# The broadcast of 1/l in a fused attention and gated-scan kernel, issued from ScalarE's queue instead of SyncE's

## What is computed

```python
x = x + attention(layernorm(x))      # x: 32 batches, 256 tokens, 128 channels
x = x + scan_ffn(layernorm(x))

# attention: 16 heads of 64, 4 persistent keys and values ahead of the 256
h = rms_norm(x) * norm_weight
q, k, v = split(h @ w_qkv.T)
q, k = rope(q), rope(k)
scores = einsum('bhid,bhjd->bhij', q, concat(pm_k, k)) * 64 ** -0.5
attn = softmax(where(causal, scores, min))
out = einsum('bhij,bhjd->bhid', attn, concat(pm_v, v)) @ w_out.T

# scan_ffn: the 32 batches are the steps of a scan
f, i = sigmoid(x_t @ wf.T + c @ uf.T + bf), sigmoid(x_t @ wi.T + c @ ui.T + bi)
c = f * c + i * tanh(x_t @ wc.T + c @ uc.T + bc)
h = tanh(x @ wo.T + c_final @ uo.T + bo)
```

## Time and profile before

| | us |
|---|---|
| median of three runs | 1159.35 (1157.94 to 1163.04) |
| the profiled execution | 1162.89 |
| its span, first to last instruction | 1161.0 |
| TensorE busy in it | 1088.0 (94%) |
| VectorE busy | 951.9 (82%) |
| ScalarE busy | 707.2 (61%) |
| GpSimd busy | 649.2 (56%) |

### The profile page before, as it was taken

The page is one execution under the profiler, slowest core; times in us unless marked ns, Lnnn a source line. Parts: engine busy times, 40 slices in busy tenths (PEclk is TensorE's granted clock), DMA queues, the critical chain, the costliest instruction groups (busy, mean ns, idle before and its releaser), DMA issues.

```text
span 1161.0 us, 47269 instructions
## 1 busy us (share of the span) xinstructions
PE 1088.0 (94%) x18411; PEld 826.2 (71%) x18411; DVE 951.9 (82%) x3304; ACT 707.2 (61%) x1603; POOL 649.2 (56%) x828
## 2 busy tenths in 40 slices
PE   4879999999999999999999999999999999999981
PEld 2557777777777777777777777777777777777671
DVE  6678888888878988888888888888888888888646
ACT  3556666666556566656666666666666566666634
POOL 3545555556555555655555565555646555655415
PEclk8799999999999999999999999999999999999995
DMA  6213333332333333233333323333332233333205
GB/s 204 93 71 99 112 112 112 112 112 77 96 110 107 113 112 99 90 98 112 105 112 113 110 86 93 110 112 113 112 112 90 85 108 108 108 107 107 72 2 145
DMA packets 78031, 120.52 MB, mean 104 GB/s; under 512 B 13041, under 2 KB 35954, under 8 KB 77682
## 3 DMA queue, kind: packets, MB, share of 16 engines
q1 hardware_dynamic: 68722, 111.21, 31.3%
q10 hardware_dynamic: 9088, 6.29, 2.0%
HBM read 41.56 MB, written 8.78 MB: 43 GB/s over the span
## 4 chain that ended last, share of the span: by engine, by line
PE 57%; DVE 15%; DMA 14%; SPq 5%; issue 4%; POOL 4%; ACT 2%; DVEq 0%; POOLq 0%; ACTq 0%
PE bank_pv L1081 10%; DMA rope_c<-rope_b 10%; PE bank L974 9%; PE bank_st L1037 7%; PE bank_sum L1118 6%; PE bank_sum L1102 4%; PE bank_sm L1013 4%; DMA linv_scratch<-linv 3%; DVE masked L781 3%; PE bank L996 3%; SPq L298 2%; DVE linv L804 2%; PE bank L993 2%; PE bank L1204 2%; PE bank L1206 2%
## 5 line engine op out<-in xcount | busy, mean ns | idle before, releaser
L396 POOL TENSOR_TENSOR qk<-rope_a,rope_c 128x512 f32<-128x512 f32 x256 | 340.7, 1331 | 304.8 <-DMA rope_c<-rope_b 300.8
L781 DVE CUSTOM_DVE_ANT_0 masked<-bank_sm,mask_q 128x132 bf16<-128x132 f32 (+1 forms) x1024 | 307.6, 356 | 44.2 <-PE bank_sm L1013 43.4
L389 POOL TENSOR_TENSOR prob<-prob 128x264 f32<-128x264 f32 x256 | 212.0, 828 | 157.6 <-ACT prob L535 150.7
L535 ACT ACTIVATE prob<-bank_st 128x784 f32<-128x784 f32 x256 | 210.3, 822 | 115.3 <-PE bank_st L1046 114.3
L770 DVE TENSOR_TENSOR rope_a<-bank,cos 128x512 f32<-128x512 f32 x256 | 174.3, 681 | 102.1 <-PE bank L974 74.6
L520 ACT ACTIVATE qk_h<-qk 128x512 f16<-128x512 f32 x256 | 160.2, 626 | 128.9 <-POOL qk L396 128.6
L1081 PE MATMUL bank_pv<-prob,v_sb 128*64 128x256 f32 (+1 forms) x2048 | 224.7, 340 | 0.6 <-DVE raw L797 0.6
L1037 PE MATMUL bank_st<-qk 64*64 64x196 f32 (+3 forms) x4096 | 185.7, 298 | 0.1
L771 DVE TENSOR_TENSOR rope_b<-bank,sin 128x512 f32<-128x512 f32 x256 | 173.8, 679 | 0.0
L1037 PEld LDWEIGHTS bank_st<-qk 64*64 64x64 f32 x4096 | 167.3, 133 | 9.0 <-issue 0.8
L1081 PEld LDWEIGHTS bank_pv<-prob,v_sb 128*64 128x64 f32 x2048 | 124.3, 136 | 54.3 <-issue 0.8
(11 more groups left out here) (202 smaller groups left out, 1793.7 us busy)
## 6 DMA issues: line engine op xcount, KB each, us to landing
rope_c<-rope_b SPq DMA_DIRECT2D x512, 128.0 KB, 2.1
rinv<-linv_scratch SPq DMA_DIRECT2D x124, 256.0 KB, 4.5
out<-x_sb SPq DMA_DIRECT2D x16, 256.0 KB, 2.5
linv_scratch<-linv SPq DMA_DIRECT2D x62, 64.0 KB, 2.1
x_sb<-x ACTq DMA_DIRECT2D x28, 128.0 KB, 5.3
pre<-w_qkv_t ACTq DMA_DIRECT2D x1, 1024.0 KB, 5.3
v_sb<-pm_v SPq DMA_DIRECT2D x64, 8.0 KB
v_end<-v_end_scratch SPq DMA_DIRECT2D x64, 8.0 KB
```

The source lines that it names most:

```text
L389: G.tensor_tensor(prob_2[:, s % 4, :, :], prob[:, s % 4, :, 0:NT - Q1], prob[:, s % 4, :, C0 + Q1:SCOL], ALU.add).then_inc(S["prob_added"], 1)
L396: G.tensor_tensor(qk[:, s, :].rearrange("p (u n) -> p u n", u=2)[:, :, 0:NT], rope_a[:, (NPAIR * j + s) % 3, :].rearrange("p (u n) -> p u ...
L535: A.activation(prob[:, s % 4, :, :], ps_st[:, :, 0:SCOL], ACT.Exp).then_inc(S["exp_done"], 1)
L781: ins = V.tensor_tensor_reduce(masked[:, e, c0:c0 + n], ps_sm[:, e, c0:c0 + n], mask_q[:, c0:c0 + n], 1.0, LOWEST, ALU.add, ALU.max, top[: ...
```

## The change

`spread_linv` is taken out of SP's list, where it stood between `swap(j, 2)` and `swap(j, 3)`, and put into ACT's list in the same iterations, behind the exponential of step 2 and ahead of `raw_copy` of step 1. It waits for the same two semaphores and issues the same four DMAs to the same tiles. SP keeps `store_linv` and the swaps. Two increments of a counter between SP's waits go away.

```diff
@@ SP
-            def spread_linv(cj):
-
-                sp.wait_ge(S["linv_stored"], 32 * (cj + 1))
-                sp.sem_inc(S["sp_tick"], 1)
-                wait(sp, S["norm_done"], 4 * cj)
-                sp.sem_inc(S["sp_tick"], 1)
-                for half in range(2):
-                    for e in range(2):
-                        src = linv_dram[e:e + 1, 2 * half:2 * half + 2, :, :].rearrange("o k b n -> o (k b n)")
-                        sp.dma_start(rinv[OWN[e], 4 * half:4 * half + 4, :].rearrange("p s n -> p (s n)"),
-                                     src.to_broadcast([64, 4 * NT])).then_inc(spread[half], 16)
...
                     if a:
                         swap(j, s)
-                    if c and s == 2 and j - 2 < NB - 1:
-                        spread_linv(j - 2)
@@ ACT
+            def spread_linv(cj):
+
+                act.wait_ge(S["linv_stored"], 32 * (cj + 1))
+                wait(act, S["norm_done"], 4 * cj)
+                for half in range(2):
+                    for e in range(2):
+                        src = linv_dram[e:e + 1, 2 * half:2 * half + 2, :, :].rearrange("o k b n -> o (k b n)")
+                        act.dma_start(rinv[OWN[e], 4 * half:4 * half + 4, :].rearrange("p s n -> p (s n)"),
+                                      src.to_broadcast([64, 4 * NT])).then_inc(spread[half], 16)
...
                     if b:
                         exp(j - 1, s)
+                    if c and s == 2 and j - 2 < NB - 1:
+                        spread_linv(j - 2)
```

## The result

| | before | changed |
|---|---|---|
| median of four runs, us | 1160.73 (1157.94 to 1163.04) | 1305.24 (1302.37 to 1308.82) |
| profiled execution, its span, us | 1162.89, 1161.0 | 1302.37, 1300.5 |
| mean granted TensorE clock | 0.976 | 0.933 |
| TensorE busy | 94% | 87% |

What follows compares the result with a forecast made beforehand. The prediction took TensorE's own work as the bound, with no slack to ACT's chain. To 1162.89 us it added 113 for the wait and 45 for the clock, less 10: 1311, or 1307 from the median; it said 1308, range 1245 to 1350.

Steps and rivals of the forecast that it cites:

- What bounds the kernel: TensorE's own work, with 15.5 us of large waits; no slack between ACT's chain in step 2 and TensorE in step 3.
- ACT's shift: ACT's chain behind the exponential of step 2 moves by 3.64 us in the mean, costing 31 x 3.64 = 113 us.
- the prediction's own signs: TensorE's scores_for_max would wait for ACT's top_t 30 times, 3.2 to 4.9 us each, about 110 us in sum.
- The clock: TensorE's granted clock falls to half behind the new wait in 25 of 31 batches, 1.8 us each: 45 us.
- Rival (a): The new wait of TensorE without loss of the clock: 1263 us, or 1239 with cheap issues; chance 0.22.
- The waits given back: Of TensorE's 15.5 us of waits for xn and h_lo, 10 come back, between 0 and 16.
- Part 1, the swap: Without the spread on SP, step 3's swap goes out up to 2 us earlier and may land some 3 us sooner.
- the two rules weighed there: DMA engines take turns between queues: swap lands about 3 us earlier; several issuing engines save only sequencer time: the delay alone.
- Rival (c): The swap behind the spread is the true bound and ACT's part is hidden: faster, about 1144 us; chance 0.03.
- Rival (d): ACT hands over DMAs beside its compute, only 1/l arrives late: shift 1.2 us, about 1190 us; chance 0.04.

Runs made afterwards that it cites:

- experiment 1: Kernel before, with one wait for linv_stored added on ACT behind the exponential of step 2, SP still issuing the spread: 1189.4 us, 1.024.
- experiment 4: Changed kernel with 54 matmuls nobody reads added on TensorE ahead of its wait for the copy of the maxima, iterations 2 to 31: 1261.66 us, 1.085.
- experiment 2: Changed kernel with ACT's four DMAs reading a constant row of weights, without the wait for 1/l: 1238.97 us, 1.065.
- experiment 3: Changed kernel with the DMAs divided: ACT waits and issues the first two, SP issues the other two as before: 1252.19 us, 1.078.
- experiment 10: Changed kernel with first_norm moved in ACT's list from the end of step 2 to the end of step 3: 1275.9 us, 1.094.
- experiment 6: Kernel before without the spread: 1/l not read back, rinv set to ones once, divide not waiting for it: 1164.71 us, 1.0018.
- experiment 5: Changed kernel with the spread moved in ACT's list to behind copy_top in step 3: 1163.9 us, 1.0006 against the kernel before.
- experiment 9: Changed kernel with the spread behind raw_copy, hi and first_norm, directly ahead of copy_top: 1240.89 us, 1.065.
- experiment 8: Kernel before with the spread divided: SP issues two DMAs ahead of swap(j, 3), ACT the other two behind copy_top: 1192.89 us, 1.025.

## Why the prediction was right, and where not

**What bounds the kernel** held. TensorE's path runs through ACT's chain of step 2, and the distance of 0.14 us in the earlier trace rows was the row that told: experiment 1 puts 33.7 us in and gets 32.7 out.

**ACT's shift** was put at 3.64 us: 2.04 until 1/l is stored, 2.40 for the issues, less 0.80. Measured in the changed kernel, over the 31 spreads: first issue at 1.82 us, issues 2.42 us, `raw_copy` at 4.29 us, a shift of 3.49 us. The issues on ACT cost what SP's cost, and the low bound from the load of x, 0.374 us each, was wrong for this shape; they took 0.62 in the median. The first term was 0.2 us smaller: 1.82 in the mean and 2.8 at the most, against 2.04 and 3.3. The factor was wrong by one. Only 30 iterations have both a spread and a `scores_for_max` (the prediction's own signs say 30 times), so that 3.64 us would have made 109, not 113; measured are 102.4 us in the 30 new waits (30 x 3.49 = 105).

**The clock** was put at 45 us with 25 falls of 1.8 us. There were 30 at the new waits, and what is left of the 140 us, less 102 for the new wait and plus 10 for waits given back, is some 47 us, 1.6 us a fall. Experiment 4 says 44 or more. The choice between the waits of 2.00 and 4.26 us of the earlier trace rows, by nearness, came out right for waits of 3.4 us. But that the wait of 2.00 us had not cost the clock was chance and no safe point to reckon from: in experiment 2 waits of 1.97 us did. Experiments 2, 3 and 10 fill the gap. Rival (a) is experiment 4's time, 1261.7 us against its 1263, but only with TensorE kept busy.

**The waits given back**, -10 us, came out as -10.1, but that is luck, as the reason was wrong. I had them from the earlier swap. Experiment 6 removes all that the spread costs the swap, and those waits stay at 15.4 us; experiment 5 hands the swap over early too and keeps 13.6. Why they go in the changed kernel no run shows. That VectorE, GpSimd and ACT's later work catch up while TensorE stands still would fit it and experiment 4 (1.9 us left), but the length of the new wait alone doesn't decide: experiment 1, with 32.7 us of wait for the copy, has 8.1 us of them left, experiments 3 and 9, with 67.5 and 65.4, have 14.4 and 14.7.

**Part 1, the swap**, failed in its size as well. The hand-over came earlier as forecast, 0.16 us behind its data instead of 1.04 in the mean. The landing did not: 5.85 us from issue to landing, against 5.82 before, though the 1 MB is now on another queue than the swap. So of "some 3 us sooner" only the 0.9 us of the hand-over are left. Of the two rules weighed there, the one that issuing from several engines saves only the issuing time (the Trainium skill, DMA: Bandwidth & Descriptors, "Issuing engines are not separate DMA queues") describes this transfer; experiment 8 shows the same engines shared.

**Rival (c)**, the swap as the true bound, fell with experiment 6: its `swap(j, 3)` is through 3.7 us earlier, the share of `rope_c`'s DMAs in the chain that ended last falls from 9.9% to 4.4%, and the time stays the same. The 14% of DMA in the earlier trace rows was no measure of what TensorE had to wait for. Rival (d) fell with the 0.80 us that became 4.29.

No version beats the kernel before: 5 and 6 equal it, and 6 shows that nothing is to be had from the spread's place. What the 15 us of waits for `xn` and `h_lo` come from stays open.

## What to carry to other kernels

Before a DMA is moved to a compute engine's queue, find the next thing on that engine that the bounding engine waits for, and read its slack from the two rows (the end of the one, the start of the other), not from the sum of waits, which is near zero as long as the two are just level. The price is the time until the DMA's own wait is over plus its issues, less the compute that the queue has already handed out ahead; put behind the needed instruction instead of ahead of it, the same DMA cost nothing and went out 0.2 us later. And a new wait of TensorE can have a second price, the clock behind it: in these runs rarely at waits of 1 us in the mean, in some iterations at 2, in all at 3.4, where it was almost half of the wait once more.

## What the runs showed of the hardware

A DMA that stands in ACT's list behind compute is issued while that compute is still running or waiting its turn: 1.80 us behind the exponential with four groups of instructions between them, and 0.57 us before the copies ahead of it began (experiment 5). Four DMAs of 256 KB took 2.42 us to issue from ACT and 2.50 us from SP, alike, and 2.84 us from ACT in experiment 2, for a reason that stays open. A swap of 256 KB took 5.82 us in the mean to land beside 1 MB on its own queue, 5.85 us beside 1 MB on another queue, and 3.07 us without it (experiment 6). 54 matmuls of 120 columns, with their weights loaded anew each time, took 3.00 us.
